# Layer stage of a six-layer transformer: the feed-forward norm with tokens on partitions, the attention mask in two half-array matmuls, and the weighted values right behind the scores

## The reference, cut to what matters

```python
def attn_layer(x, Wqkv, qs, ksc, Wo):        # 16 heads of 64, window 32
    q, k, v = split(x @ Wqkv)
    q = l2norm(q) * qs;  k = l2norm(k) * ksc
    q = q*cos*scale + rotate_half(q)*sin*scale
    k = k*cos*inv   + rotate_half(k)*sin*inv
    return local_attention(q, k, v) @ Wo     # a query sees keys 0 to 32 back
...
mask = (it < jb) | (it > jb + w) | (jb == -1)
sim = where(mask, -max, einsum(q, k) * 8.0); attn = softmax(sim)
...
def ffn_layer(x, g, bln, W1, b1, W2, b2):
    mu = x.mean(-1);  var = ((x - mu) ** 2).mean(-1)
    xn = (x - mu) / sqrt(var + 1e-05) * g + bln
    a, gate = split(xn @ W1 + b1)            # 341 hidden columns each
    return a * gelu(gate) @ W2 + b2
for i in range(6):
    x = attn_layer(shift_tokens(x), ...) + x
    x = ffn_layer(shift_tokens(x), ...) + x
```

## Time and profile before

| what | value |
|---|---|
| runs | 4807.0, 4807.64, 4809.76 us; median 4807.64 us |
| span of the profiled execution | 4809.0 us (no time of its own is listed for it; the three runs lie from 2.0 below to 0.8 us above this span) |
| PE busy | 4210.8 us (88%), 74016 matmuls |
| DVE busy | 3900.8 us (81%) |
| ACT, POOL busy | 3381.0 us (70%), 2752.5 us (57%) |
| layer stage | about 1700 us to the end, 192 tiles |

### The profile page before, as it was taken

One profiled execution on the slowest core, in us unless ns is written; L12 is line 12 of the kernel. 1 busy time (PEld: TensorE's weight loads), 2 busy tenths in 40 slices (PEclk: granted clock), 3 DMA queues, 4 the chain that ended last, 5 costly groups with the idle time before them and its releaser, 6 DMA issues. The chain is left out here.

```text
span 4809.0 us, 192113 instructions
## 1 busy us (share of the span) xinstructions
PE 4210.8 (88%) x74016; PEld 3351.0 (70%) x74017; DVE 3900.8 (81%) x6510; ACT 3381.0 (70%) x5947; POOL 2752.5 (57%) x3197
## 2 busy tenths in 40 slices
PE   7898875697454799999999999999999999999996
PEld 4444432375231688888887888888887888788884
DVE  5777757643446899999999999989999999999996
ACT  4555521254223688978997898879987898889994
POOL 3222213634221777767776777767776777677771
PEclk9999977798776999999999999999999999999997
DMA  3000003252210211121111211121112111121110
GB/s 150 1 0 0 0 0 118 88 200 77 95 59 19 67 44 48 41 63 46 47 48 51 57 43 48 42 65 42 48 43 59 47 48 44 40 67 45 48 43 30
DMA packets 141883, 255.16 MB, mean 53 GB/s; under 512 B 34160, under 2 KB 56944, under 8 KB 137072
## 3 DMA queue, kind: packets, MB, share of 16 engines
q1 hardware_dynamic: 133520, 235.49, 16.7%
q0 software_dynamic: 8192, 17.84, 1.3%
HBM read 70.76 MB, written 44.04 MB: 24 GB/s over the span
## 5 line engine op out<-in xcount | busy, mean ns | idle before, releaser
L2522 POOL TENSOR_TENSOR d_rc<-d_rc,d_rs 128x512 f32<-128x512 f32 x768 | 963.6, 1276 | 473.4 <-DVE d_rs L2605 459.1
L2532 POOL TENSOR_TENSOR d_rc<-d_rc,d_inv 128x1024 f32<-128x1024 f32 x384 | 722.9, 1903 | 121.2 <-DVE d_inv L2626 120.9
L2088 PE MATMUL d_pair<-d_W_high,d_xs_high 128*128 128x512 f32 x1152 | 519.0, 451 | 122.4 <-DVE d_W_low L2591 42.5
L2605 DVE TENSOR_TENSOR d_rc<-d_pair,d_rot 128x512 f32<-128x512 f32 x768 | 528.1, 688 | 89.1 <-ACT d_sq L2337 72.6
L2337 ACT ACTIVATE d_sq<-d_pair 128x512 f32<-128x512 f32 x768 | 435.2, 597 | 139.0 <-PE d_pair L2088 133.9
L2605 DVE TENSOR_TENSOR d_rs<-d_pair,d_rot 128x512 f32<-128x512 f32 x768 | 523.0, 681 | 0.0
L2088 PE MATMUL d_pair<-d_W_low,d_xs_high 128*128 128x512 f32 x1152 | 461.0, 400 | 1.5 <-issue 1.5
L2088 PE MATMUL d_pair<-d_W_high,d_xs_low 128*128 128x512 f32 x1152 | 461.5, 401 | 0.4 <-issue 0.4
L2615 DVE TENSOR_REDUCE d_ss<-d_sq 128x16 f32<-128x1024 f32 x384 | 448.3, 1210 | 0.0
L2235 PE MATMUL d_pair<-d_OT,d_Wo 128*128 128x128 f32 x3072 | 383.6, 279 | 0.0
L2132 PE MATMUL d_pair<-d_ident,d_rc 128*128 128x128 f32 x3072 | 368.2, 273 | 1.0 <-ACT d_sq L2337 1.0
(11 more groups left out here) (370 smaller groups left out, 11146.5 us busy)
## 6 DMA issues: line engine op xcount, KB each, us to landing
d_VW<-d_V SPq DMA_DIRECT2D x768, 128.0 KB, 2.4
d_VW<-d_V SPq DMA_DIRECT2D x576, 64.0 KB, 2.0
leaf_rows<-a_zeros SPq DMA_DIRECT2D x12, 1152.0 KB, 14.7
q_xrow<-leaf_rows SPq DMA_DIRECT2D x24, 576.0 KB
leaf_out<-q_yrow SPq DMA_DIRECT2D x24, 512.0 KB
d_W_whole<-Wqkv_dram SPq DMA_DIRECT2D x7, 1536.0 KB, 6.7
f_xrow<-leaf_rows SPq DMA_DIRECT2D x8, 576.0 KB, 3.7
b_table<-q_w_dram SPq DMA_DIRECT2D x4, 1024.0 KB, 8.6
```

The source lines that it names most:

```text
L2088: mm = nc.tensor.matmul(target, x_part[:, t.par, :], w_part[:, c, :], start=n == 0, stop=n == 2)
L2522: nc.gpsimd.tensor_tensor(own[:, :, a, :], own[:, :, a, :], other[:, :, 1 - a, :], ALU.add).then_inc(s[f"add{qk}_ready"], 1)
L2532: nc.gpsimd.tensor_tensor(heads(rc[:, t.par, half, :]), heads(rc[:, t.par, half, :]), inv[:, t.par, half, :].unsqueeze(2).to_broadcast([12 ...
L2605: ins = nc.vector.tensor_tensor(heads(target), heads(ps[:, j, :]), rot[:, t.par, half, cs, :].unsqueeze(1).to_broadcast([128, HP, DH]), AL ...
```

## The change

It has three parts.

1. **Norm.** `centred` swaps its two operands, so that the centred tile has tokens on partitions. ACT's square adds up along the row (`accum_out`) into one number per token; the variance matmul is gone. The root (`deviation`) and the reciprocal work on 128x1, the product on DVE is a `tensor_scalar`. The result `xh` must be turned back: a new PE stage `normalised_turned` (L2254) transposes it into the centred bank, and ACT's `normalised` reads it from PSUM. `xn` has two buffers. In ACT's order `deviation` goes ahead of the squares of k1, and `normalised` ahead of the copy of the turned queries.
2. **Mask.** One bank's mask matmul used all 128 rows (`ident_b` times a 128-row mask). Now each of the two banks has a matmul over 64 rows, one in the upper and one in the lower half of the array.
3. **Order on PE.** v0 is computed ahead of `hidden_gate`, and `attend` comes directly behind the scores.

```diff
-                nc.tensor.matmul(centred_bank[:, 0:128], centre[:], xs2[:], start=True, stop=True).then_inc(s["mean_done"], 1)
+                nc.tensor.matmul(centred_bank[:, 0:128], xs2[:], centre[:], start=True, stop=True).then_inc(s["mean_done"], 1)
...
-            def variance(t):
-                wait(pe, "xsq_ready", t)
-                wait(pe, "on_ready", t, 2)
-                nc.tensor.matmul(var_bank[:, 0:128], mean_w[:], xsq[:], start=True, stop=True).then_inc(s["var_done"], 1)
+            def normalised_turned(t):
+                wait(pe, "xh_ready", t)
+                nc.tensor.transpose(centred_bank[:, 128:256], xh[:], ident[:]).then_inc(s["xht_done"], 1)
...
                 for odd in range(2):
-                    nc.tensor.matmul(s_pair[:, odd, :], ident_b[:], mask[:, t.par, :].unsqueeze(1).to_broadcast([128, HP, DH]),
+                    half = slice(64 * odd, 64 * odd + 64)
+                    nc.tensor.matmul(s_pair[:, odd, :], mask_rows[half, t.par, :], mask[half, :].unsqueeze(1).to_broadcast([64, HP, DH]),
...
 # PE, queries_turned
-                wait(pe, "std_ready", t, -4)
 # PE, attention_turned
-                wait(pe, "xh_ready", t, -2)
+                wait(pe, "xn_ready", t, -2)
 # PE, slot
                 values(tile(1), 1)
-                variance(tile(5))
                 project(tile(4))
+                normalised_turned(tile(5))
                 queries_turned(tile(1))
                 keys_turned(tile(1))
                 hidden_up(tile(6))
                 attention_turned(tile(3))
                 probabilities_turned(tile(2))
+                values(tile(0), 0)
                 hidden_gate(tile(5))
                 scores(tile(1))
-                values(tile(0), 0)
                 attend(tile(2))
 # ACT
-                nc.scalar.activation(xsq[:], centred_bank[:, 0:128], ACT.Square).then_inc(s["xsq_ready"], 1)
+                nc.scalar.activation(xsq[:], centred_bank[:, 0:128], ACT.Square, accum_out=xsq_sum[:]).then_inc(s["xsq_ready"], 1)
-                nc.scalar.activation(std[:], var_bank[:, 0:128], ACT.Sqrt, bias=eps[:, 0:1]).then_inc(s["std_ready"], 1)
+                nc.scalar.activation(std[:], xsq_sum[:], ACT.Sqrt, bias=eps[:, 0:1], scale=1.0 / 128).then_inc(s["std_ready"], 1)
-                wait(act, "xh_ready", t)
-                nc.scalar.activation(xn[:], xh[:], ACT.Identity, bias=vecs_n[:, 1:2], scale=vecs_n[:, 0:1]).then_inc(s["xn_ready"], 1)
+                wait(act, "xht_done", t)
+                nc.scalar.activation(xn[:, t.par, :], centred_bank[:, 128:256], ACT.Identity, bias=vecs_n[:, 1:2], scale=vecs_n[:, 0:1]).then_inc(s["xn_ready"], 1)
 # DVE, layernorm
-                wait(dve, "xn_ready", t, -1)
-                nc.vector.tensor_tensor(xh[:], centred_bank[:, 0:128], rstd[:], ALU.mult).then_inc(s["xh_ready"], 1)
+                wait(dve, "xht_done", t, -1)
+                nc.vector.tensor_scalar(xh[:], centred_bank[:, 0:128], rstd[:, 0:1], None, ALU.mult).then_inc(s["xh_ready"], 1)
```

More of the change, by code:

```diff
@@ L1844, in local_attention_layers @@
         rot = sb("d_rot", [128, 2, 2, 2, DH])
-        mask = sb("d_mask", [128, 2, DH], BF16)
-        ident_b = sb("d_ident_b", [128, 128], BF16)
+        mask = sb("d_mask", [128, DH], BF16)
+        mask_rows = sb("d_mask_rows", [128, 2, 128], BF16)
         ident = sb("d_ident", [128, 128])
         centre = sb("d_centre", [128, 128])
-        mean_w = sb("d_mean_w", [128, 128])
         eps = sb("d_eps", [128, 1])
@@ L2246, in centred, with hidden @@
                     wait(pe, "xh_ready", t, -1)
[L2247 to L2249 removed]
+                nc.tensor.matmul(centred_bank[:, 0:128], xs2[:], centre[:], start=True, stop=True).then_inc(s["mean_done"], 1)
+            def normalised_turned(t):
                 if not t.live:
                     return
[L2252 to L2258 removed]
+                wait(pe, "xh_ready", t)
+                nc.tensor.transpose(centred_bank[:, 128:256], xh[:], ident[:]).then_inc(s["xht_done"], 1)
+            def hidden(t, W1, ps, done):
                 for c in range(HCH):
[L2260 removed]
+                    mm = nc.tensor.matmul(ps[0:HROWS[c], 128 * c:128 * c + 128], W1[:, 128 * c:128 * c + HROWS[c]], xn[:, t.par, :],
                                           start=True, stop=True)
@@ L2405, in squares_centred @@
                 wait(act, "mean_done", t)
-                wait(act, "var_done", t, -1)
-                nc.scalar.activation(xsq[:], centred_bank[:, 0:128], ACT.Square).then_inc(s["xsq_ready"], 1)
+                wait(act, "std_ready", t, -1)
+                nc.scalar.activation(xsq[:], centred_bank[:, 0:128], ACT.Square, accum_out=xsq_sum[:]).then_inc(s["xsq_ready"], 1)
             def load_sqrt(t):
@@ L2456, in slot @@
                 squares(tile(1), 1, "k", 0)
+                normalised(tile(6))
                 take_queries_turned(tile(2))
                 take_keys_turned(tile(2))
-                normalised(tile(6))
                 take_attention_turned(tile(4))
@@ L2741, in constants @@
             rotary[:, par, half_, 1] = sin[rows] * sign * s[rows]
-    query = np.arange(128)[:, None] % WIN
+    query = np.arange(WIN)[:, None]
     slot = np.arange(2 * WIN)[None, :]
     seen = (slot >= query) & (slot <= query + WIN)
-    first = seen & ((np.arange(128)[:, None] >= WIN) | (slot >= WIN))
-    mask = np.where(np.stack([first, seen], 1), 0.0, -1e30).astype(mybir.dt.np(BF16))
+    first = seen & (slot >= WIN)
+    mask = np.tile(np.where(np.concatenate([seen, first]), 0.0, -1e30), (2, 1)).astype(mybir.dt.np(BF16))
+    tokens = np.arange(128)
+    row_of = np.stack([tokens % WIN + np.where(tokens < WIN, WIN, 0), tokens % WIN])
+    rows = np.tile((np.arange(2 * WIN)[:, None, None] == row_of[None]).astype(np.float32), (2, 1, 1)).astype(mybir.dt.np(BF16))
     centre = np.eye(128, dtype=np.float32) - np.float32(1.0 / 128)
-    return {"ident": np.eye(128, dtype=np.float32), "rotary": rotary, "window_mask": mask, "centre": centre}
+    return {"ident": np.eye(128, dtype=np.float32), "rotary": rotary, "window_mask": mask, "window_rows": rows, "centre": centre}
 def layouts_d(i):
```

34 lines of the change are left out of this document (17 added, 17 removed).

## The result

The changed kernel takes 4855.98 us in the median of four runs (4848.66 to 4862.25); the kernel before, run beside it, 4808.7. The ratio is 1.0101, with a 95% interval of 1.0087 to 1.0116: slower by 47 us. The prediction was 4850 us and slower. The time is right; the trace says that its split is not. The trace is of the slowest of the four runs (4862.25 us).

A forecast was written before the change was run, and what follows sets the result against it. PE alone bounds the kernel before; the change closes a PE-DVE ring through `xh`. Slot 8.67 + 7.49 = 16.16 us, +0.27 over 180 slots, +48.6 less 5 at layer starts: 4850 us, range 4812 to 4890.

The forecast's parts named there:

- The two chains are one ring: PE waits for DVE's `xh`, DVE for PE's next scores: slot 16.16 us against 15.89, +0.27.
- v0's 0.70: PE's three v0 matmuls, 0.70 us, move from behind the scores to between turned queries and first score, where DVE waits.
- M to q1's rotary products: On DVE, from M, the start of L2633, 2.70 us to L2660 and 1.13 to the next instruction; wait for ACT's squares goes.
- from there to the reciprocal: On DVE, from q1's rotary products to the norm's reciprocal: 4.00 us, taken as all unchanged work.
- handing over, weight load and transpose: From DVE's `xh` to PE's turned queries: 0.07 us handoff, 0.11 uncovered weight load, 0.11 transpose.
- PE's idle time of 0.8 and 0.4 us at L2254: PE waits for `xh` in front of the new transpose, 0.8 and 0.4 us in the two kinds of slot.
- That gives back about 1 us in each of five layers: In a layer's first slot DVE, 0.9 us late for the scores, would be in time: 5 us gained in all.
- ACT's wait for the turned queries: On ACT `normalised` falls into this wait and gives `xn` earlier than today; no size given.
- (a): PE stays the bound, never held by DVE's product: 15.49 us a slot, 4731 us; chance 0.10.
- (b): Balance: mask 0.12 and handoffs 0.13 us less give a slot of 15.91, no change, 4807 us; chance 0.08.
- (c): PE's two mask matmuls run one after the other, plus the mode change: 0.18 us more a slot, 4883 us; chance 0.15.
- (d): POOL's sine products hold DVE's new `tensor_scalar`, making it 1.1 us late: +200, 5050 us; chance 0.04.

The follow-up runs named there:

- the dose: Changed kernel with DVE's product of the norm computed twice, first into a spare tile, so `xh` comes 0.26 us later: 4882.77 us, 1.0158 to the kernel before.
- order alone: Kernel before with only v0 moved ahead of the gate half and `attend` right behind the scores, old norm and mask: 4801.65 us, 0.9984.
- order on top of the new norm: Changed kernel (4855.98 us) against the same kernel with v0 put back behind the scores, new norm and mask kept (4806.85 us, 0.9995).
- the runs with the wait removed: Changed kernel with the transpose of `xh` one stage later on PE (4787.1 us), or with DVE's reciprocal and product ahead of k0's rotary products (4790.34 us).

## Why the prediction was right, and where it was not

*The kind of bound: right.* "The two chains are one ring" holds: PE idles in front of L2254, DVE's wait for the scores rose, the two kinds of slot became alike (15.89 and 15.98), and the dose of 0.26 us came through whole. "v0's 0.70 has moved from a part of PE's time that ran beside DVE to the part that DVE waits for" is what the runs show: order alone -7, order on top of the new norm +49. What it adds to a slot is less than v0's time, though (0.19 of 0.79), because v0 was not wholly beside DVE before: it stood ahead of q1.

*The ring's length: 0.23 too long.* By its terms:

| term | predicted | measured |
|---|---|---|
| M to q1's rotary products | 3.83 | 3.82 |
| from there to the reciprocal | 4.00 | 3.85 |
| reciprocal and gap | 0.26 | 0.18 and 0.28, in turn |
| product to its end | 0.29 | 0.35 |
| handing over, weight load and transpose | 0.29 | 0.23 |
| turned queries to the first score | 5.97 | 5.94 |
| first score to M | 1.52 | 1.52 |

The step that failed is "from there to the reciprocal are 4.00 (3014.04), all of it unchanged work". It was not all work. The step from the feed-forward add to the next rotary row was 0.39 us before (3011.25 to 3011.64) and is 0.26 now (2987.91 to 2988.17): a short wait with no idle note in the row, for q0 (before, q0's last matmul ended just 0.04 us ahead of this row), which PE now delivers earlier. I took the same kind of wait out in front of q1 and left this one in. That is 0.15 of the 0.23; the rest is the handing over (0.06 less), the gap ahead of the product in every other slot and the last part of PE, against the product itself (0.06 more). With 0.27 a slot, 0.2 too much were multiplied by 180.

*PE's idle time of 0.8 and 0.4 us at L2254: too large.* By the starts it is 0.46 and 0.23, because `xh` comes earlier (the step above) and PE later, with small waits of 0.05 us in front of `down` and v1 in the slots without the branch.

*"That gives back about 1 us in each of five layers": wrong, also in sign.* DVE did come in time for the scores of the slot that it splits the weights in, the prediction's "first slot" and the third of the nine (it took 0.4 to 1.7 us less in four of the five layers), but the second and the eighth slot lost far more: +33.1 us over the 45 slots. The prediction had both causes before its eyes. It set `normalised` into "ACT's wait for the turned queries" without asking what else `normalised` waits for in a layer's first tile, and what is queued behind it on ACT; and it looked for stalls of DVE at a layer start only in front of L2633. Whoever makes a ring must read the slots that are not steady once more, since slack that covered their stalls is gone.

So the time came out right by luck, because two errors of about 40 us cancel: +48.6 for the steady slots against +9.1 measured, -5 for the layers' starts against +33.1 and +5.7 while the pipeline fills.

*Rivals.* (a), PE stays the bound, fell: the slot of 15.49 needs `xh` at M + 7.7 to 8.1, and its end was at M + 8.20 to 8.29. It missed by little; the runs with the wait removed have a slot of 15.52 to 15.63. (b), balance, was nearest to the steady slots, but not to the time. (c) fell: the two half-array masks ran side by side (one row of 0.39 us for both), 0.32 to the first score, and are worth 0.12 us a slot, against 0.09 predicted. (d) fell: no product took more than 0.35, with POOL at its sine products.

## What to carry to other kernels

Before moving an operation of one engine in front of another's, write down the ring that this closes, and take everything else out of it: the same three matmuls of v0 gained 7 us with the old norm and cost 49 inside the ring. If a result comes a few tenths too late, give it one stage more (two lines, 65 to 69 us). And cost a moved wait twice, once in a steady slot and once in the first tile of a layer, where the instruction also waits for that layer's loads, with everything that is queued behind it.

## What the hardware showed that I had not expected

- The clock is part of the price of a stall: in the slot from 3126 to 3148 the two idle stretches cost 3.7 us, and the granted clock of 0.85 added 3.1 to PE's busy time. Slots of the same place with the same waits and a clock of 1.00 took 19.3 us instead of 22.4. The clock fell although no idle stretch of PE ahead of it was longer than 1.9 us. What decides between the two is open.
- Two mask matmuls of 64 rows each show as one row of 0.39 us for both, the duration of one alone.
- DVE's product with one scalar per row takes 0.35 us for 128x128 from PSUM, more than the product with a whole second tensor (0.29 in the earlier trace rows).
- The accumulating square of ACT brings a second instruction, the read of the sum, which takes 0.19 us. It stayed in ACT's slack.
- DVE and ACT stand 1.3 to 2.5 us in front of the first instruction of their slot where the loop over the layers jumps back, with nothing shown that they wait for. When another instruction was put in that place the stall stood in front of it; what it is stays open, and no run removed it.
